# Wide attention on one core: the order at its two ends, and the values' projection ahead of the weighted sum

## The reference, cut to what matters

```python
def _L1_attn_ref(x, Wq, Wk, Wv, Wo):     # 32 heads, 8 kv heads, HEAD_DIM 128, T 512
    q = jnp.einsum('bth,oh->bto', x, Wq)...; k = ...Wk; v = ...Wv
    q = q * cos + _rotate_half(q) * sin
    k = k * cos + _rotate_half(k) * sin
    scores = jnp.einsum('bkgtd,bksd->bkgts', qg, k) * scale
    scores = jnp.where(causal, scores, -jnp.inf)
    attn = jax.nn.softmax(scores, axis=-1)
    out = jnp.einsum('bkgts,bksd->bkgtd', attn, v)
    ...
    return jnp.einsum('bto,ho->bth', out, Wo)
...
x = _layernorm(x + _L0_ffn_ref(x, ...), axis=-1)
x = _layernorm(x + _L1_attn_ref(x, ...), axis=-1)
x = _layernorm(x + _L1_ffn_ref(x, ...), axis=-1)
```

## Time and profile before

| | us |
|---|---|
| median of 3 runs | 2006.45 (2006.06 to 2009.45) |
| the profiled execution | 2006.38 |
| its span in the trace | 2004.7 |
| TensorE busy | 1894.5 (95% of the span) |
| VectorE, ScalarE, GpSimd busy | 1140.3, 858.7, 868.8 |
| wide attention, from the release of its stage to the first `gate_up` behind it | 315.1 to 1130.3 |

### The profile page before, as it was taken

One profiled execution on the slowest core, in us unless ns is written; L12 is line 12 of the kernel. 1 busy time (PEld: TensorE's weight loads), 2 busy tenths in 40 slices (PEclk: granted clock), 3 DMA queues, 4 the chain that ended last, 5 costly groups with the idle time before them and its releaser, 6 DMA issues.

```text
span 2004.7 us, 29837 instructions
## 1 busy us (share of the span) xinstructions
PE 1894.5 (95%) x11008; PEld 1288.1 (64%) x11008; DVE 1140.3 (57%) x2177; ACT 858.7 (43%) x1896; POOL 868.8 (43%) x1380
## 2 busy tenths in 40 slices
PE   6999988999999999999999799999999998999998
PEld 3544446888888888888887687864444454544455
DVE  5676466666666666666666424235556355566465
ACT  1565544444444444444444333323555402565441
POOL 2454325545454545454544344323344312443352
PEclk9999988999999999999999899999999989999999
DMA  6113000101010101010100234203223003111101
GB/s 215 40 34 110 1 11 1 54 1 53 1 53 1 54 1 53 1 53 1 53 1 32 80 104 152 80 7 90 57 57 107 33 1 80 34 34 44 51 10 43
DMA packets 46211, 94.61 MB, mean 47 GB/s; under 512 B 7689, under 2 KB 35721, under 8 KB 43145
## 3 DMA queue, kind: packets, MB, share of 16 engines
q1 hardware_dynamic: 43474, 90.34, 13.7%
q10 hardware_dynamic: 2592, 2.36, 0.5%
HBM read 61.68 MB, written 2.10 MB: 32 GB/s over the span
## 4 chain that ended last, share of the span: by engine, by line
PE 78%; DVE 11%; ACT 5%; issue 3%; POOL 1%; DMA 1%; PEld 0%; SPq 0%; PEldq 0%; POOLq 0%; ACTq 0%; DVEq 0%
PE PS L1540 9%; PE PS L1440 9%; PE PS L463 6%; PE PS L566 6%; PE PS L1962 5%; PE PS L544 5%; PE PS L510 5%; PE PS L591 4%; PE PS L1518 4%; PE PS L1975 3%; PE PS L1469 3%; PE PS L1502 3%; PE PS L478 2%; PE PS L1933 2%; PE PS L512 2%
## 5 line engine op out<-in xcount | busy, mean ns | idle before, releaser
L990 ACT ACTIVATE PB<-PS 128x512 f32<-128x512 f32 x480 | 280.9, 599 | 236.5 <-PE PS L544 233.5
L897 POOL TENSOR_SCALAR_AFFINE_SELECT PB<-PB 128x256 f32<-128x256 f32 (+1 forms) x480 | 173.3, 365 | 320.2 <-ACT PB L990 313.9
L769 DVE TENSOR_REDUCE NM<-PS 128x2 f32<-128x1024 f32 x192 | 209.2, 1092 | 168.5 <-PE PS L512 167.2
L510 PE MATMUL PS<-KQ 96*128 96x512 bf16 (+3 forms) x768 | 185.3, 306 | 17.4 <-DVE NM L769 10.9
L544 PE MATMUL PS<-KQ 99*128 99x512 bf16 (+3 forms) x768 | 183.2, 304 | 4.8 <-ACT PB L990 3.4
L1856 POOL TENSOR_SCALAR PR<-PR,RCP 128x512 f32<-128x512 f32 (+3 forms) x256 | 134.3, 533 | 105.2 <-DVE RCP L1651 105.0
L1664 DVE TENSOR_REDUCE NX<-PS 128x1 f32<-128x512 f32 (+3 forms) x256 | 125.0, 488 | 79.9 <-PE PS L1491 74.0
L463 PE MATMUL PS<-XTT,WA 128*128 128x512 f32 x288 | 145.3, 611 | 13.5 <-DVE ident_masks_b L2597 12.0
L1726 ACT CAST OTH<-PS 128x512 fp32r<-128x512 f32 x64 | 37.6, 587 | 279.3 <-PE PS L1523 279.3
L1790 ACT ACTIVATE PR<-PS,NX 128x512 f32<-128x512 f32 (+3 forms) x256 | 137.2, 536 | 29.8 <-DVE NX L1664 25.8
L512 PE MATMUL PS<-ident_masks_b 128*128 128x128 bf16 x768 | 149.2, 223 | 0.0
(11 more groups left out here) (331 smaller groups left out, 4617.9 us busy)
## 6 DMA issues: line engine op xcount, KB each, us to landing
KQ<-HI SPq DMA_DIRECT2D x90, 128.0 KB, 2.4
KQ<-MID SPq DMA_DIRECT2D x72, 128.0 KB, 2.4
WB<-f_w SPq DMA_DIRECT2D x12, 768.0 KB, 4.3
WB<-w1o SPq DMA_DIRECT2D x8, 1024.0 KB, 7.9
WC<-f_w SPq DMA_DIRECT2D x10, 768.0 KB, 4.4
WB<-w1a SPq DMA_DIRECT2D x8, 768.0 KB, 4.4
WB<-w1b SPq DMA_DIRECT2D x8, 768.0 KB, 5.9
WA<-w SPq DMA_DIRECT2D x6, 1024.0 KB, 6.3
```

What stands on the lines that cost most here:

```text
L510: pe.matmul(ps, KQ[0:SR, self.query(G, h), i * P:(i + 1) * P], KQ[0:SR, self.key(G, h), 0:n], start=True, stop=False)
L769: x = dve.tensor_reduce(nm[:, h:h + 2, i], PS[:, b:b + 2, 0:(i + 1) * P], AX.X, ALU.max, negate=True)
L897: pool.affine_select(blocks, blocks, [[0, count], [1, P]], ALU.is_ge, 0.0, base=0, channel_multiplier=-1).then_inc(s16["probs_ready"].sem, 1)
L990: act.activation(PB[:, n % PBS, :], PS[:, 4 + n % 2, :], ACT.Exp, scale=self.scale)\
```

## The change

Nothing is computed differently; instructions change their place in the queues.

1. In the loop over heads `project_v(u+1)` stands in front of `weighted(n-1)` in h = 2, not behind it.
2. First end: `Ffn0.tensor` issues `begin_high(0)`, `begin_low(0)`, then `begin_high(1)`, `begin_low(1)`. `rope(0)` moves into `Ffn0.vector`, in front of the stage's end. `rope(2)` on VectorE, `rope_high(2)` on ScalarE and `rope_low(2)` on GpSimd move from inside head 0 to in front of it.
3. Other end: `weighted(63)` moves in front of `turn` 2 and 3 on TensorE, `high_o(63)` in front of `take` 2 and 3 on ScalarE, and `finish` 2 and 3 behind the four `low_pT` on VectorE.

```diff
                     if n == 8:
                         a1.project_v(pe, 0, (2, 3))
-                    if n in (8, 9):
-                        a1.begin_high(pe, n - 8)
+                    if n == 8:
+                        a1.begin_high(pe, 0)
+                    if n == 9:
+                        a1.begin_low(pe, 0)
                     if n >= 2:
...
-                for p in (0, 1):
-                    a1.begin_low(pe, p)
+                a1.begin_high(pe, 1)
+                a1.begin_low(pe, 1)
...
                 dve.wait_ge(self.tails[1].s_x.sem, self.tails[1].s_x.at(NT))
+                dve.wait_ge(s1_tab.sem, 16)
+                a1.rope(dve, 0)
...
+                    if h == 2 and u + 1 < NU:
+                        self.project_v(pe, u + 1)
                     if n:
                         self.weighted(pe, n - 1)
                     if h == 1 and u + 1 < NU:
                         for _ in self.project(pe, 5 * u + 5):
                             pass
-                    if h == 2 and u + 1 < NU:
-                        self.project_v(pe, u + 1)
...
                     self.transpose_probs(pe, n, i)
+                self.weighted(pe, n)
                 for t in range(2, NT):
                     pe.wait_ge(self.tails[0].s_t.sem, self.tails[0].s_t.at(t - 1))
                     self.tails[0].turn(pe, t, PS[:, t % 2, :])
-                self.weighted(pe, n)
                 self.output(pe, NU - 1)
...
             def vector(self, dve, st):
-                dve.wait_ge(s1_tab.sem, 16)
-                self.rope(dve, 0)
                 self.rope(dve, 1)
                 self.rope_low(dve, 0)
                 self.take_v(dve, 0)
                 self.rope_low(dve, 1)
+                self.rope(dve, 2)
...
-                        if n == 0 and i == 1:
-                            self.rope(dve, 2)
...
-                last.finish(dve, 2)
-                last.finish(dve, 3)
                 self.take_o(dve, GQ * NU - 2)
                 for i in range(NT):
                     self.low_pT(dve, GQ * NU - 1, i)
+                last.finish(dve, 2)
+                last.finish(dve, 3)
                 self.take_o(dve, GQ * NU - 1)
...
                 self.x_high(act, 1)
-                for p in range(2):
+                for p in range(3):
                     self.rope_high(act, p)
...
-                        if n == 0 and i == 2:
-                            self.rope_high(act, 2)
...
                 for i in range(NT):
                     self.copy_pT(act, GQ * NU - 1, i)
+                self.high_o(act, GQ * NU - 1)
                 for t in range(2, NT):
                     self.tails[0].take(act, t, PS[:, t % 2, :])
-                self.high_o(act, GQ * NU - 1)
...
                 for p in range(3):
                     self.sum(pool, p)
+                self.rope_low(pool, 2)
...
-                    if n == 0:
-                        self.rope_low(pool, 2)
```

## The result

| | before | after |
|---|---|---|
| median, us | 2006.26 (2006.0 to 2009.45, 4 runs) | 1985.39 (1982.18 to 1986.79, 4 runs) |
| ratio | | 0.9889, interval 0.9874 to 0.9905 |
| the profiled execution, its span | 2006.38, 2004.7 | 1984.74, 1983.0 |

The kernel is faster by 20.9 us. The forecast was 1983.1, so 2.3 us of the gain are missing; the time lies in the range (1980.5 to 1988.5), a little above the likeliest case's own end of 1985. In the listing after, the lines have moved: scores are L1490 (were L1486), the projection ahead L1444, `project_v` L1473, `weighted` L1522, `output` L1544, the exponential L1791, `rope_low` L1609, `low_pT` L1623, the down matmuls of `Ffn1` L1973.

What follows compares the result with a forecast made beforehand. TensorE, busy 95% of the span, bounds the kernel; time is won only where it waits or runs at lower clock. 12.0 + 5.6 + 5.7 = 23.3 us off 2006.38 makes 1983.1, range 1980.5 to 1988.5.

Steps and rivals of the forecast that it cites:

- likeliest case: Whole kernel: the forecast itself, 1983.1 us, alone from 1981 to 1985, chance 0.63.
- Part 1: Middle, h = 2: `project_v` covers `weighted`'s wait of 0.73 and saves a 0.08 restart, 0.81 a group: 12.0 us.
- The rival that the wait only moves: Middle: ScalarE is late in h = 3, TensorE waits as in h = 2, the move gives nothing: 1995.1 us, chance 0.08.
- GpSimd's low part stays ahead of h = 3 by 0.8 us: Scores of h = 3, groups with long low part of output weights: low part 1.6 us ahead of TensorE, 0.8 remains.
- Part 2: First end: earlier `rope_low(2)` lets head 1 start 4.25 earlier and run faster; `weighted(0)` 5.7 earlier, taken as 5.6 us.
- rival of the lower clock: Either end: granted clock falls to 0.50 once, costing 1.5 to 3 us: 1985.5 us, chance 0.17.
- a sign of being wrong: First end: a granted clock of 0.5 between 322 and 330 would show the prediction wrong.
- the 7.2 us of an h = 2: First end, head 1: takes 7.2 us like an h = 2, two short waits included, where it took 8.69 before.
- Part 3: Other end: `low_pT` goes ahead of the blocked `finish`, so the transposes, `weighted(63)` and `output` start earlier: gain 5.7 us.
- The rival of a held `low_pT`: Other end: GpSimd holds `low_pT` or the transposes after all, the gain there is 1.5 us: 1987.3 us, chance 0.07.
- the 1.5 named: Other end, sign of being right: no TensorE wait above 1.5 us from the first third transpose block to `output`.
- everything behind shifts as it is: Behind the other end: the stage's release, the loads of `Ffn1`'s weights and all that follows move earlier unchanged.

Runs made afterwards that it cites:

- e4_h3: The kernel before with `project_v` in front of `weighted` in h = 3 and no longer in h = 2: 2042.22 us, ratio 1.0177.
- e1_middle: The kernel before with only `project_v` moved in front of `weighted` in h = 2, both ends as before: 1997.24 us, ratio 0.9952.
- e7_v_first: The changed kernel with `take_v(0)` in front of `rope_low(0)` on VectorE at the first end: 1983.56 us, ratio 0.9893.
- after_again: The changed kernel measured once more, with no edit: 1985.48 us against 2004.83, ratio 0.9899.
- e5_no_lock: The kernel before with GpSimd's low part of `Ffn1`'s first weights issued behind its four low parts of x: 2002.94 us, ratio 0.9984.
- e6_chunk: The changed kernel with two quarters of the projection ahead issued in step 1 of h = 2, none in step 3: 1975.58 us, ratio 0.9855.
- e8_scales: The changed kernel with `Ffn1`'s two loads of scales ahead of its two 768 KB weight loads in SP's queue: 1979.67 us, ratio 0.9866.
- e10_dve_only: The kernel before with `finish` 2 and 3 behind the four `low_pT` on VectorE, TensorE and ScalarE in old order: one execution, 2000.72 us.
- e2_first: The kernel before with only the first end's new order: 1999.82 us, ratio 0.9968.
- e3_last: The kernel before with only the other end's new order: 2000.51 us, ratio 0.997.

## Why the prediction was right, and what it missed

**Part 1, 12.0 predicted, 11.5 to 11.9 measured.** The step by which it was sized holds: from the first scores of h = 2 to the second matmul of the first scores of h = 3 it took 12.89 us, and takes 12.09, 0.80 less, where 0.81 was worked out. TensorE after, the counterpart of the earlier trace rows:

```profile
583.29 0.39 PE L1490 MATMUL PS<-kH,qH 128*128 128x512 f32 x1
...
589.55 0.39 PE L1444 MATMUL PS<-XLa,A1H 128*128 128x512 f32 x1
...
593.27 0.49 PE L1522 MATMUL PS<-PTH,VH 128*128 128x512 f32 x1
...
595.15 0.40 PE L1490 MATMUL PS<-kH,qH 128*128 128x512 f32 x1
595.38 0.39 PE L1491 MATMUL PS<-kL,qH 128*128 128x512 f32 x1
```

`weighted` follows without a wait, and the scores of h = 3 run on at 0.23 us: one restart instead of two. The rival that the wait only moves is refuted by e1_middle, which shows no wait in h = 3. What I argued in one sentence, that GpSimd's low part stays ahead of h = 3 by 0.8 us, turned out to be what the whole place of `project_v` hangs on: e4_h3 took that cover away and paid 2.3 us a group on average.

**Part 2, 5.6 predicted, 6.1 measured, by a way that was partly wrong.** Right: the release of the stage came 0.4 later (0.45 predicted), and the first exponential and the end of head 0 came where I had put them. In the time of before, that is with the 1.25 us of the column ahead of it added, they are 324.8 (predicted 324.8) and 327.9 (predicted 327.9). Wrong: what lies between. I had put the end of `project(2)` at 318.5 and the first scores at 320.9, and didn't count the idle time between them. It is there in TensorE after, and the clock falls behind it:

```profile
319.63 0.78 PE L1490 MATMUL PS<-kH,qH 128*128 128x512 f32 x1 [2.03 <-DVE qL L1609]
```

The scores and projection steps up to 322.9 ran at 0.51, which took up the time in which TensorE would have waited 1.8 us for the exponential: the slow matmuls were free, since their successor had to wait anyway. e7_v_first shows the other course, full clock and the wait of 1.59. Under either, head 0 ends when the exponential lets it. So the rival of the lower clock came about in its condition and not in its price at this end, and this stretch, which the prediction listed as a sign of being wrong, did no harm. The blocked low part of the keys took 1.43 us (1.53 in the earlier trace rows). The half us more than predicted comes from head 1: I gave it the 7.2 us of an h = 2, and it took 6.6 (326.66 to 333.25) with a single wait of 0.37, as its copies were not late.

```profile
330.71 0.39 PE L1490 MATMUL PS<-kH,qH 128*128 128x256 f32 x1 [0.37 <-ACT PR L1791]
...
333.25 0.40 PE L1522 MATMUL PS<-PTH,VH 128*128 128x512 f32 x1
```

**Part 3, 5.7 predicted, 5.8 measured** (5.0 in after_again, where the rival of the lower clock did take its price, 0.9). VectorE, GpSimd and TensorE after, the counterparts of the earlier trace rows:

```profile
1090.38 1.02 DVE L1623 TENSOR_TENSOR PTL<-PS,PTH 128x384 fp32r<-128x384 f32 x2 [0.18 <-ACT PTH L1720]
1091.93 0.62 DVE L1623 TENSOR_TENSOR PTL<-PS,PTH 128x256 fp32r<-128x256 f32 x2 [0.53 <-ACT PTH L1720]
1092.47 1.92 DVE L269 TENSOR_SCALAR XBB<-XBB,mv,rstd 128x512 f32<-128x512 f32 x2
...
1090.19 3.46 POOL L2089 TENSOR_TENSOR B1L<-WB,B1H 128x1536 fp32r<-128x1536 f32 x1
...
1091.08 0.77 PE L1506 MATMUL PS<-ident_masks,PR 128*128 128x128 f32 x3 [1.14 <-DVE PTL L1623]
1095.73 0.51 PE L1544 MATMUL PS<-Wo1H,OTH 128*128 128x512 f32 x1 [0.53 <-DVE OTL L1644]
```

All four `low_pT` lie inside the GpSimd operation (1090.19 to 1093.65) and take 1.02 and 0.62 for two each, unblocked. The two `finish` behind them take 1.92 for two, from 1092.47: they wait for its end and are done at 1094.39, before ScalarE has what `take_o` needs. The rival of a held `low_pT` is refuted. The longest wait on the way is 1.14, under the 1.5 named. A share of the gain is clock, which the prediction didn't name: before, TensorE stood at 0.50 from 1109.4 to 1116.0, under the wait of 5.39 and the matmuls behind it, and after, this end ran at full clock. The Trainium skill ("SBUF — State Buffer", section Who interferes with whom) says that a VectorE instruction in a 2-port mode and a GpSimd instruction exclude each other, as do one with two SBUF inputs and a GpSimd instruction that reads SBUF, and that one with at most one SBUF input outside these modes doesn't contend. By that rule the trace agrees in this place too, and e5_no_lock puts its price here at 3.2 us.

**What was missed, 2.3 us.** The parts gave 23.5 us in the profiled execution (6.13 + 11.53 + 5.81), 0.2 more than their sum of 23.3; that it fits so well is partly luck, for part 1 gave 0.5 less and part 2 0.5 more than predicted. Against the later runs of the kernel before (2004.83), the changed kernel run again gained 19.4 and not 20.9, so that up to 4 us are missing. And that the median lies at 1985.4, beside the 1985.5 of the rival of the lower clock, is chance: the loss lies where that rival had no term. The step that failed is the sentence that everything behind shifts as it is. In the profiled execution two pieces didn't:

The first, -1.49, lies ahead of the last `weighted`. Behind TensorE's short waits in head 62 the clock stood at 0.51 from 1077.4 to 1080.8, the fourth row of the stretches above. The kernel run again has the same waits (1.12 us at the third scores in both) and full clock in that place:

```profile
1073.00:1081.00 8.00, 5.98 (x39) 4.67 (x38) 5.28 (x17) 5.99 (x16) 3.06 (x5) 1.00 0.00 0
```

None of the other kernels lost time in this piece (e4_h3 has only its `project_v` there). So it is a matter of the single execution, and not of the order.

The second, -1.6 to -3.1, lies in the head of `Ffn1`, and it came in all four profiled executions with the three parts and the old order of the loads (the changed kernel twice, e6_chunk, e7_v_first). The first activation hangs there on the landing of the scales f_ad, a load of 256 KB queued behind two of 768 KB. ScalarE and TensorE before:

```profile
1147.38 0.69 ACT L2016 ACTIVATE SG<-PS,AGU 128x512 f32<-128x512 f32 x1 [5.13 <-DMA WB<-f_ad]
...
1150.38 0.50 PE L1975 MATMUL PS<-B1H,HH 128*128 128x512 f32 x1 [0.86 <-DVE HL L2058]
```

After, and then the same kernel again:

```profile
1124.18 0.69 ACT L2014 ACTIVATE SG<-PS,AGU 128x512 f32<-128x512 f32 x1 [5.17 <-DMA WB<-f_ad]
...
1127.18 0.50 PE L1973 MATMUL PS<-B1H,HH 128*128 128x512 f32 x1 [1.94 <-DVE HL L2056]
```

```profile
1129.02 0.79 PE L1973 MATMUL PS<-B1H,HH 128*128 128x512 f32 x1 [4.04 <-DVE HL L2056]
```

ScalarE waits as long as before, but TensorE has come to its down matmuls with 1.94 and 4.04 us to wait instead of 0.86, and the clock falls behind it (0.51 in 1128.6 to 1132, above). Up to that matmul nothing is lost in the profiled execution: it starts 23.20 us earlier than before, as much as all the pieces ahead give (23.23). The 1.56 are lost in the slow stretch behind it. In the kernel run again 0.6 are lost up to it and 2.5 behind. Before, the wait was short because the matmuls ahead of it ran at 0.50 and took up the time:

```profile
1140.00:1146.80 6.80, 5.71 (x14) 4.49 (x15) 0.00 (x0) 2.23 (x2) 3.46 (x1) 0.50 0.91 310
```

So the transfer, issued with the release of the stage, sets when the down matmuls begin, and TensorE's work ahead of them is free to be slow or fast. e8_scales takes the cause away:

```profile
1119.79 0.69 ACT L2014 ACTIVATE SG<-PS,AGU 128x512 f32<-128x512 f32 x1 [2.61 <-DMA WB<-f_ad]
...
1123.05 0.40 PE L1973 MATMUL PS<-B1H,HH 128*128 128x512 f32 x1
```

ScalarE's wait halves, TensorE's is gone, and the piece turns from -1.6 to +2.4. That the scales hold this piece is shown. Why it lost against before is shown for the profiled executions only. Over all kernels with the old order of the loads the loss goes with the clock behind the first down matmul: 1.6 to 3.1 where it fell (the changed kernel twice, e1_middle, e6_chunk, e7_v_first, e10_dve_only), and 0.1 to 0.3 where it stayed full (e2_first, e3_last, e4_h3, e5_no_lock). The wait alone doesn't decide it: it was 2.21 in e3_last, without a fall, and 1.94 in the changed kernel, with one. That it belongs to the new order is not shown, since e1_middle, whose end is that of the kernel before, lost 2.2 as well. Whether the kernel before loses as much on average stays open, as do the reasons for which a slow stretch comes behind one wait of 1 to 2 us and not behind another.

## What to carry to other kernels

On a TensorE that is 95% busy a short wait is worth more than its bracket says: read it from start to start against the same matmuls without it (0.56 shown was 0.81 here, 0.26 was 0.53), and cover it with independent matmuls moved ahead of it by a few instructions. Ask of every block that is moved what it covers where it stands, and which load or buffer it releases; moving it to the next head instead cost 36 us. And where an engine's work behind a seam hangs on a transfer issued at the seam, the smaller loads that are needed first go first in the queue.

## What the hardware showed that I had not expected

- Slow matmuls in front of a wait are free: 3.3 us at 0.51 from the first scores on replaced a wait of 1.59 us at full clock, and head 0 ended at the predicted time.
- Waits of 1 to 2 us may or may not be followed by a stretch at 1.2 GHz: 1.12 in head 62 was in one execution of the changed kernel and not in another; 2.03 at the first scores was, 1.48 wasn't; 1.94 at the down matmuls was, 2.21 there in another kernel wasn't. The one in head 62 cost 1.5 us.
- Executions of one kernel differ by more than any part of an end: 2000.7 to 2011.4 us over 20 of the kernel before, and up to 5.4 us of lead came about in code that no edit touched.
